# The first pair of sequences in the order of the second: one attention alone, the other inside the first expert block

## The reference

```python
x = x + attn_a(norm(x))      # 16 heads, causal, keys and values through a 128-wide latent (silu)
x = x + moe(norm(x))         # 8 experts as low-rank additions to one MLP, two chosen per token
x = x + attn_b(norm(x))      # 16 x 16 attention among the heads of one token, with rope
x = x + moe(norm(x))
x = x + delta(norm(x))       # gated delta rule, 6 heads
x = x + ffn(norm(x))         # 256 -> 1024 -> 256, gelu
x = x + attn_c(norm(x))      # 16 query heads, one key head, causal
x = x + ffn(norm(x))
```

## Time and profile before

| | |
|---|---|
| median of three runs | 1569.86 us (1567.25 to 1571.34) |
| profiled execution, its time | 1570.56 us |
| profiled execution, its span | 1568.8 us |
| mean granted clock of TensorE | 0.89 of full |
| PE, PEld busy | 84%, 64% of the span |
| DVE, ACT, POOL busy | 48%, 27%, 5% of the span |

### The profile page before, as it was taken

One profiled execution on the slowest core, in us unless ns is written; L12 is line 12 of the kernel. 1 busy time (PEld: TensorE's weight loads), 2 busy tenths in 40 slices (PEclk: granted clock), 3 DMA queues, 4 the chain that ended last, 5 costly groups with the idle time before them and its releaser, 6 DMA issues.

```text
span 1568.8 us, 17406 instructions
## 1 busy us (share of the span) xinstructions
PE 1311.2 (84%) x6780; PEld 998.9 (64%) x6780; DVE 746.1 (48%) x1631; ACT 419.9 (27%) x910; POOL 79.6 (5%) x69
## 2 busy tenths in 40 slices
PE   5689987986988798877877999879779887897878
PEld 4567563744857678665666766547458576786656
DVE  4533286585445454224233335855943453633241
ACT  2522020111322241334242521111113222413251
POOL 0000000000110110000000000000001102100000
PEclk9889998997999779689987999979979998896898
DMA  9000000000000000000000000000000000000000
GB/s 377 3 1 0 0 1 0 0 1 0 1 1 1 1 1 1 0 1 1 7 8 1 1 0 1 1 0 0 0 0 1 1 0 1 1 1 1 1 1 14
DMA packets 3264, 16.97 MB, mean 11 GB/s; under 512 B 240, under 2 KB 2288, under 8 KB 2544
## 3 DMA queue, kind: packets, MB, share of 16 engines
q10 hardware_dynamic: 1008, 13.77, 2.1%
q1 hardware_dynamic: 2176, 2.10, 0.4%
HBM read 14.82 MB, written 1.05 MB: 10 GB/s over the span
## 4 chain that ended last, share of the span: by engine, by line
PE 61%; DVE 25%; ACT 8%; issue 4%; POOL 1%; DMA 0%; DVEq 0%; ACTq 0%; POOLq 0%
PE bank L612 56%; DVE scr L1657 4%; ACT scr L1167 3%; DVE scr L1658 2%; DVE scr L1641 2%; DVE scr L1640 2%; PE bank L619 2%; DVE scr L1697 1%; PE bank L987 1%; DVE scr L1583 1%; ACT scr L1145 1%; DVE stat L1424 1%; DVE X L1417 1%; DVE scr L1625 1%; POOL rstd L1956 1%
## 5 line engine op out<-in xcount | busy, mean ns | idle before, releaser
L612 PE MATMUL bank<-pack,scr 128*128 128x256 f32 (+2 forms) x944 | 339.1, 515 | 5.2 <-ACT scr L1145 5.2
L612 PE MATMUL bank<-XnT,pack 128*128 128x256 f32 x1024 | 273.6, 412 | 17.7 <-ACT XnT L1145 10.6
L612 PEld LDWEIGHTS bank<-pack,scr 128*128 128x128 f32 x944 | 191.1, 209 | 138.1 <-issue 111.6
L612 PE MATMUL bank<-scr,pack 128*128 128x256 f32 x944 | 242.1, 399 | 30.7 <-DVE scr L1583 25.5
L612 PEld LDWEIGHTS bank<-XnT,pack 128*128 128x128 f32 x1024 | 208.7, 208 | 57.0 <-ACT XnT L1145 13.7
L612 PEld LDWEIGHTS bank<-scr,pack 128*128 128x128 f32 x944 | 186.0, 200 | 63.0 <-DVE scr L1583 28.7
L1145 ACT ACTIVATE scr<-bank 128x512 f32<-128x512 f32 (+7 forms) x112 | 49.0, 454 | 284.6 <-PE bank L619 182.9
L1583 DVE TENSOR_TENSOR scr<-bank,scr 128x256 f32<-128x256 f32 x112 | 45.7, 422 | 165.7 <-ACT scr L1214 165.1
L619 PE MATMUL bank<-pack,scr 128*128 128x128 f32 x232 | 43.1, 319 | 89.1 <-DVE scr L1609 25.0
L1417 DVE TENSOR_TENSOR X<-bank,X 128x512 f32<-128x512 f32 x32 | 22.1, 692 | 185.6 <-PE bank L612 185.5
L612 PE MATMUL bank<-scr 32*128 32x128 f32 (+4 forms) x944 | 101.7, 374 | 8.6 <-DVE scr L1871 4.7
(11 more groups left out here) (175 smaller groups left out, 1462.9 us busy)
## 6 DMA issues: line engine op xcount, KB each, us to landing
pack<-pack_dram ACTq DMA_DIRECT2D x1, 6408.0 KB, 17.9
pack<-pack_dram ACTq DMA_DIRECT2D x1, 2052.0 KB, 30.4
pack<-pack_dram ACTq DMA_DIRECT2D x1, 1595.0 KB, 25.0
pack<-pack_dram ACTq DMA_DIRECT2D x1, 1361.0 KB, 7.4
X<-x SPq DMA_DIRECT2D x4, 256.0 KB, 7.9
pack<-pack_dram ACTq DMA_DIRECT2D x1, 1024.0 KB, 20.0
out_dram<-X SPq DMA_DIRECT2D x4, 256.0 KB, 2.1
pack<-pack_dram ACTq DMA_DIRECT2D x1, 657.5 KB, 26.0
```

Of the source, the lines that this page charges most:

```text
L612: return pe.matmul(o, l, r, start=start, stop=stop, skip_group_check=True)
```

## The change

The first pair gets the order of the second. Only the keys of sequence 0 are made first. Its attention of four units is streamed alone, and `norm_t`, `latent`, `kv` and `kv_fold` of sequence 1 stand beside it, at places -1, 0, 1 and 2. After `out_in`, `out_proj`, the norm and the router of sequence 0, a new function `first_experts` runs the expert block of sequence 0 with the whole attention, output projection, norm, router and spread of sequence 1 between its matmuls, and with the banks split by `halves`. `angles` moves from slot 2 of that block to slot `f1`. The second pair calls the same function with the order that it had.

```diff
-            for s in range(S):
-                stage("norm_t", 0, s)
-                stage("latent", 0, s)
-            for name in ("kv", "kv_fold"):
-                for s in range(S):
-                    stage(name, 0, s)
-            stream(stage, units(0, 0) + units(0, 1),
-                   {5: [("out_in", 0, 0)], 6: [("out_proj", 0, 0), ("norm_x", 1, 0)], 7: [("norm_t", 1, 0)]})
-            for other in (("router", 0, 0), ("out_in", 0, 1), ("spread_t", 0, 0), ("out_proj", 0, 1),
-                          ("spread", 0, 0), ("norm_x", 1, 1)):
+            for name in ("norm_t", "latent", "kv", "kv_fold"):
+                stage(name, 0, 0)
+            stream(stage, units(0, 0), {-1: [("norm_t", 0, 1)], 0: [("latent", 0, 1)], 1: [("kv", 0, 1)],
+                                        2: [("kv_fold", 0, 1)]})
+            for other in (("out_in", 0, 0), ("out_proj", 0, 0), ("norm_x", 1, 0), ("norm_t", 1, 0), ("router", 0, 0)):
                 stage(*other)
-            experts(stage, 0, 0, {1: [("norm_t", 1, 1)], 2: [("angles", 0, 0)], 3: [("router", 0, 1)],
-                                  5: [("spread_t", 0, 1)], 6: [("spread", 0, 1)]})
+            first_experts(stage, 0, 1, {"f1": [("angles", 0, 0)]})
             middle(stage, 0, 1)
...
+        def first_experts(stage, c, d, more):
+
+            halves[0] = True
+            for other in (("scores", 0, (d, 0)), ("spread_t", 0, c), ("spread", 0, c)):
+                stage(*other)
+            beside = {"f0": [("weights", 0, (d, 0))],
+                                  "f1": [("values", 0, (d, 0)), ("scores", 0, (d, 1))],
+                                  "f2": [("values_t", 0, (d, 0))], 2: [("weights", 0, (d, 1))],
+                                  "f3": [("values", 0, (d, 1)), ("scores", 0, (d, 2))],
+                                  3: [("values_t", 0, (d, 1))], "f4": [("weights", 0, (d, 2))],
+                                  4: [("values", 0, (d, 2)), ("scores", 0, (d, 3))],
+                                  "f5": [("values_t", 0, (d, 2))], 5: [("weights", 0, (d, 3))],
+                                  "f6": [("values", 0, (d, 3))], 6: [("values_t", 0, (d, 3))],
+                                  7: [("out_in", 0, d)], 8: [("out_proj", 0, d), ("norm_x", 1, d)],
+                                  "down00": [("norm_t", 1, d), ("router", 0, d)], "down01": [("spread_t", 0, d)],
+                                  "down10": [("spread", 0, d)]}
+            for slot, stages in more.items():
+                beside[slot] = beside.get(slot, []) + stages
+            experts(stage, 0, c, beside)
+            halves[0] = False
```

More of the change, by code:

```diff
@@ L451, in program @@
                 stage(*other)
[L452 to L466, removed]
+            first_experts(stage, c, d, {})
             middle(stage, c, d)
```

## The result

The changed kernel takes 1583.14 us (median of four runs, 1580.67 to 1585.05) against 1569.57 us for the kernel before beside it: a ratio of 1.0086, with a 95% interval of 1.0067 to 1.0106. The forecast was 1581.3. The profiled execution has a span of 1581.4 us, 12.6 more than before.

A forecast was written before the change was run, and what follows sets the result against it. The chain of waits was 61% TensorE and 25% DVE. `lora_t` of sequence 0 at 182.6 + 4.0 = 186.6 against 175.17, 11.4 us later, gave 1570.56 + 11.4 = 1582.0 profiled, 1581.3 median; range 1574 to 1589.

The forecast's parts named there:

- two waits: Unit 1's scores wait for unit 0's exponentials, a loss of 2.8 us; `x_first(3)` waits behind `angles`, 4.0 us.
- Part 1: Front of the kernel: sequence 0's keys run alone, first scores at 23.15 in place of 29.54, a gain of 6.4 us.
- Part 2: First scores to first `values`: units 0 and 1 share banks 0 to 3, 10.9 us in place of 8.14.
- Part 3: Rest of sequence 0's attention: periods 18.0 us, bank waits 2.0, one low-clock period 1.4; attention ends at 57.8.
- three bank waits: Attention of sequence 0: latent's silu 1.0 us, `kT` and `kp` 0.5 each, 2.0 together; bounds 0 and 4.
- Part 4: Sequence 0's output projection, norm and router with nothing beside them: 1.39, 7.15 and 1.39, sum 9.9 us; router at 67.7.
- Part 5: Sequence 0's expert block, router to `lora_t`: 114.9 us taken from the second pair; `lora_t` at 182.6 without `angles`.
- Part 6: `angles` in slot `f1` delays the silu and PE before `x_first(3)` by 4.0 us; bounds 0 and 5.7.
- upper bound of 5.7: Cost of `angles` in slot `f1` if the wait sends the clock down for a stretch, 1.4 to 1.7 more.
- Behind the landmark: After the transposes of sequence 0's `lora_t`: same `middle` in both orders; clock alone can move the end 6.7 us either way.
- The rival that said the clock would help: Denser work raises the clock in the block and second pair's `middle`: up to 18.5 us gained, 1562.8; chance of faster 0.06.
- Its sum, 1584.1: Forecast with the skill's 2.66 us per table switch: `angles`' two added loads cost 5.3 in place of 2.6, 2.7 higher.

The follow-up runs named there:

- both repairs: Changed kernel with `norm_t` of sequence 1 between `kv` and `kv_fold` of sequence 0, and `angles` moved to the idle start: 1572.16 us, ratio 1.0022.

## Why the prediction was right

**The sign and its reasons** held. The forecast named two waits that the trace of before does not show. Both are in the profile after, at the place and with the releaser named (30.18 and 113.21), and undoing either takes it away. The two waits are 7.7 of the 16.8 us (4.0 and 3.7). With both undone, 14.2 are gone, since low stretches of the clock went with them.

**Part 1** (keys) was right in kind: first scores at 11.5 from the first matmul in place of 10.6. Of the 0.9, 0.8 is the latent at the low clock, 5.21 us for what took 4.40.

**Part 2** (the opening): 12.1 in place of 10.9. The chain of steps is the one forecast; the scores ran at the low level (1.62 and 1.03 us for 0.94 and 0.61), and the latent's matmuls, 2.76 us, ended last, 0.6 behind ACT's copy.

**Part 3** (the stream) was 3.6 too dear. The three bank waits show 2.5 us of idle PE, but the two full periods took 13.95 us, only 0.9 more than twice the 6.53 of the earlier trace rows, because the wait for ACT's copy ahead of `values` is gone in return; I had put 2.0. The one low stretch that I counted, 1.4, didn't come, and the last period is 3.89 and not 4.98.

**Part 4** (projection to router) was mis-sized, 16.5 in place of 12.2 with the end of the attention. I took durations from rows in which units of the other sequence ran beside these stages. Alone, they leave TensorE idle in between, and it ran at 1.2 GHz for 13.9 us. The forecast said that nothing would stand beside them then, and gave that no price. In the kernels above that leave this stretch as it is, it took between 13.5 us (both repairs, clock 0.65 from `out_proj` to the router) and 16.5, so some 1.3 us of the miss stay in the best trace, and up to 3.0 are the clock.

**Part 5** (the block taken over from the second pair) was right to 0.2 us, once `angles` is out (114.65). The 113.2 of the kernel with both repairs shows that so close an agreement is in part luck.

**Part 6** (`angles`): 6.8 in place of 4.0. The gap is 3.73. The load ahead of the sines (106.34), which I did not count, ended 0.8 us before they could start and cost nothing. The low clock behind the gap, which I left in the bounds at 1.4 to 1.7, cost 2.9. The upper bound of 5.7 was too low.

**Behind the landmark** I forecast no shift, with 6.7 either way for the clock. It was 5.1 down. So the landmark came 5.4 us later than the sum had it, while the time came within 2 us: the agreement in the time is closer than the steps deserve, because the clock gave back behind them about what they had missed. I forecast the time, and not this cancelling. The rival that said the clock would help had other places for it: the first part of the block (0.65, with 0.67 before) and the second pair's `middle` (240.65 us, with 240.64 before) gave nothing. What came back lay in the first `middle` (1.5) and in the last stretch (3.6), which it didn't name.

**The Trainium skill** ("ScalarE: Activation LUTs", What ACT_TABLE_LOAD costs) gave 2.66 us for a switch. In the changed kernel too the next activation starts 1.30 us after the start of a load (108.73 to 110.03, 110.25 to 111.55), which does not agree: there is no room for a drain. Its sum, 1584.1, came closer to the time for another reason, the low clock.

## What to carry to other kernels

A rotation of buffers that is decided while the order is written out is part of the order: one claim moved in front of a pair of units can put both on the same banks, and this can be read from the code before anything runs. Work that costs nothing in one slot can cost 6.8 us in the same slot of another order, so the price of a slot must be taken with its neighbours. Stages that lose what stood beside them can lose clock too. Where the clock dips come and go, compare kernels between landmarks inside the trace, and shift the whole program a little to see which part of a gain stays.

## What the runs showed of the hardware that was not expected

The two levels of TensorE's clock make one and the same stretch come out at two lengths: from `lora_t` to the first group of line 1697 it was 232.2 to 234.0 us in nine traces of the first pair and 240.6 or 240.8 in two, without an edit there, and 237.6 in one; at the short length the clock was 0.90, at the long one 0.87. A delay of 1.6 us at the start cost 3.3 us in one kernel, and in another 4.4 by the medians, which were taken in different groups, or 5.8 by their distances from the kernel before. Differences of 8 us are as large as the largest effect of an edit here.

Behind an exponential the sines had a table load ahead of them (106.34) and the next silu had another (107.24 without the exponential between), 1.28 us each. Behind a silu they had none: in the kernel before the silu stands at 118.48 and the sines at 123.11 with no load between. A load can also start while its activation still waits for input, and then costs nothing: the one at 106.34 ended at 107.62, and the sines started at 108.39.
